# Attention over slots: both passes by blocks of 128 rows with running states, plain fp32 products on the diagonals, and a new order of the step

## The reference

```python
q, k, v, s = x @ Wq, x @ Wk, x @ Wv, clip(x @ Ws, -32, 32)   # 64, 64, 128, 64 columns a head
z = cumlogsumexp(s, time); p = exp(s - z); g = exp(z_before - z)
hk = hk * g + k (outer) p        # running state, 64 x 64
ok = q . hk                      # one row of 64 slots for each time step
pv = softmax(ok)
hv = hv * g + p (outer) v        # running state, 64 x 128
o  = pv . hv
o  = rmsnorm(o) * weight * silu(x @ Wg);  out = o @ Wo
```

## Time and profile before

| | |
|---|---|
| Median of 3 runs | 1976.25 us (1975.31 to 1977.02) |
| Profiled execution | 1975.16 us |
| Its span, first to last instruction | 1973.3 us |
| Mean granted TensorE clock | 0.995 |
| Busy: TensorE, VectorE, ScalarE, GpSimd | 99%, 69%, 39%, 31% |
| A middle step of the attention (614.90 to 651.34 us) | 36.44 us |
| The attention | to about 1216 us of the span |

### The profile page before, as it was taken

The page is one execution under the profiler, slowest core; times in us unless marked ns, Lnnn a source line. Parts: engine busy times, 40 slices in busy tenths (PEclk is TensorE's granted clock), DMA queues, the critical chain, the costliest instruction groups (busy, mean ns, idle before and its releaser), DMA issues.

```text
span 1973.3 us, 30299 instructions
## 1 busy us (share of the span) xinstructions
PE 1944.0 (99%) x11747; PEld 1430.3 (72%) x11747; DVE 1365.7 (69%) x2203; ACT 779.2 (39%) x1915; POOL 607.5 (31%) x636
## 2 busy tenths in 40 slices
PE   8999999999999999999999998999999999999998
PEld 7887888888888888878888875444444368888886
DVE  4666666666676666666666678999999965555556
ACT  3332232233232332322322332888888842222222
POOL 2142242152152152152142234244442223323232
PEclk9999999999999999999999998999999999999999
DMA  5000100100100100000000000111111111111112
GB/s 171 1 1 12 38 1 12 38 1 11 38 1 12 38 4 23 24 11 28 11 11 4 1 6 19 28 27 26 26 27 27 24 23 26 27 23 27 22 17 86
DMA packets 124988, 47.06 MB, mean 24 GB/s; under 512 B 89264, under 2 KB 116400, under 8 KB 124848
## 3 DMA queue, kind: packets, MB, share of 16 engines
q1 hardware_dynamic: 124848, 45.14, 9.3%
HBM read 32.79 MB, written 4.19 MB: 19 GB/s over the span
## 4 chain that ended last, share of the span: by engine, by line
PE 93%; ACT 3%; DVE 3%; SPq 1%; issue 1%; DMA 0%; POOL 0%; POOLq 0%; DVEq 0%; ACTq 0%
PE a_ps L66 20%; PE a_ps L68 19%; PE a_ps L67 19%; PE a_ps L1020 6%; PE a_ps L982 5%; PE a_ps L1036 4%; PE a_ps L1163 4%; PE a_ps L1176 3%; PE a_ps L1004 3%; PE a_ps L1096 2%; PE a_ps L964 2%; PE a_ps L1099 2%; PE a_ps L1102 2%; ACT x_prob L1627 2%; PE a_ps L1181 1%; PE a_ps L1135 1%
## 5 line engine op out<-in xcount | busy, mean ns | idle before, releaser
L1691 DVE TENSOR_REDUCE a_raw_qks<-a_ps 128x1 f32<-128x512 f32 x512 | 320.9, 682 | 16.5 <-PE a_ps L982 15.7
L1627 ACT ACTIVATE x_prob<-a_ps 128x512 f32<-128x512 f32 x512 | 279.8, 608 | 62.3 <-PE a_ps L1004 60.9
L66 PE MATMUL a_ps<-a_vg_hi,a_xT_lo 128*128 128x512 f32 x512 | 205.0, 400 | 0.0
L68 PE MATMUL a_ps<-a_vg_hi,a_xT_hi 128*128 128x512 f32 x512 | 199.8, 390 | 0.0
L67 PE MATMUL a_ps<-a_vg_lo,a_xT_hi 128*128 128x512 f32 x512 | 199.6, 390 | 0.0
L791 POOL TENSOR_TENSOR a_causal<-a_causal,a_mask 128x128 f32<-128x128 f32 x32 | 14.7, 460 | 558.7 <-ACT a_causal L1520 558.7
L1743 DVE SCALAR_TENSOR_TENSOR a_gate<-a_gate,a_ps 128x256 f32<-128x256 f32 x128 | 53.8, 420 | 179.9 <-ACT a_gate L1515 179.9
L66 PE MATMUL a_ps<-a_xT_hi,a_qks_lo 128*128 128x512 f32 x384 | 157.5, 410 | 0.4 <-DVE a_xT_lo L1722 0.4
L68 PE MATMUL a_ps<-a_xT_hi,a_qks_hi 128*128 128x512 f32 x384 | 150.5, 392 | 0.0
L67 PE MATMUL a_ps<-a_xT_lo,a_qks_hi 128*128 128x512 f32 x384 | 149.5, 389 | 0.0
L982 PE MATMUL a_ps<-a_xT_lo,a_xT_hi 64*128 64x512 f32 x384 | 142.9, 458 | 2.7 <-DVE a_raw_qks L1691 1.8
(11 more groups left out here) (194 smaller groups left out, 4560.9 us busy)
## 6 DMA issues: line engine op xcount, KB each, us to landing
a_raw_vg<-in_L_attn_Wv_dram SPq DMA_DIRECT2D x8, 512.0 KB, 4.6
a_raw_vg<-in_L_attn_Wg_dram SPq DMA_DIRECT2D x8, 512.0 KB, 6.4
a_raw_qks<-in_L_attn_Wo_dram SPq DMA_DIRECT2D x8, 512.0 KB, 3.7
a_xT_lo<-a_xT_lo SPq DMA_DIRECT2D x32, 128.0 KB, 2.3
x_values<-acc SPq DMA_DIRECT2D x13, 256.0 KB, 2.8
acc<-in_x_dram SPq DMA_DIRECT2D x3, 1024.0 KB, 10.1
out_dram<-acc SPq DMA_DIRECT2D x6, 512.0 KB, 2.8
f_raw_down<-in_L_ffn_down_w_dram SPq DMA_DIRECT2D x44, 64.0 KB, 2.4
```

The source lines that it names most:

```text
L66: pe.matmul(out, w_lo, x_hi, start=start, stop=False)
L68: return pe.matmul(out, w_hi, x_hi, start=False, stop=stop)
L1627: nc.scalar.activation(prob[par][:, s % 4, :], score_bank(q, s, par), ACT.Exp, scale=X_SCALE).then_inc(exp_done[par], 1)
L1691: nc.vector.tensor_reduce(nm[:, q % 2, i % 4, par, i // 4:i // 4 + 1], max_bank(u, q, i, par), AX.X, ALU.max, negate=True).then_inc(max_re ...
```

## The change

- The first pass gets running states like the second. `key_scores` multiplies only the four diagonal blocks of keys and queries, in plain fp32, into the two banks `ch`; VectorE masks them in two operations (`mask_scores`). `key_states` multiplies the keys by rows (`key_rows`) with e for the first three blocks, 64 columns each, into `ch[0]`, and VectorE adds them up (`running_key_states`). `slots` multiplies e with the masked diagonal blocks and adds, for blocks 1 to 3, the running key state times the queries.
- For the keys by rows there are three more transposes (`transpose_keys`, into `okb`) and a copy on ScalarE (`copy_key_rows`).
- Keys and queries are kept in plain fp32 (`keep_keys`, `keep_queries`); all left and right high and low parts go.
- `diagonals` uses plain fp32 products. `eT` gets a second buffer.
- GpSimd's `mask_diagonals` and ScalarE's `copy_chunks` go.
- The order changes. TensorE in a middle step: key_scores, project S, key_states, states, slots, project VG, transposes of the normalised slots, project VG+1, out_rows, project VG+2, transposes of the softmax, project_out (four tiles), project VG+3, diagonals, project K, project Q, transposes of eT, transposes of the keys, values. VectorE puts one half of the gated output of step n-1 into step n, behind the masks, and does both halves of the reciprocal with the scan. ScalarE's copies of x in steps 0 and 1 (`high_x`) stand before the copy of VG+1; in step 1 two of the four transposes of x stand behind those of the softmax.

The core of the diff:

```diff
-S, VG, Q, K = 0, 1, 5, 6
+S, VG, K, Q = 0, 1, 5, 6
...
+            def key_scores(n):
+
+                pe.wait_ge(keys_kept, n + 1)
+                pe.wait_ge(queries_kept, n + 1)
                 wait(pe, diag_masked, n)
...
+                for i in range(TT):
+                    rows = slice(i * P, (i + 1) * P)
+                    for h in range(2):
+                        mm = pe.matmul(ch[h][:, rows], keys[HALF[h], rows], queries[HALF[h], rows], start=True, stop=True)
+                mm.then_inc(scores_done, 1)
+
+            def key_states(n):
+
+                pe.wait_ge(key_rows_ready, n + 1)
+                pe.wait_ge(e_ready, n + 1)
+                pe.wait_ge(scores_masked, 2 * n + 1)
+                for i in range(TT - 1):
+                    for h in range(2):
+                        mm = pe.matmul(ch[0][HALF[h], i * DK:(i + 1) * DK], key_rows[:, i, DK * h:DK * (h + 1)],
+                                       e[:, i, DK * h:DK * (h + 1)], start=True, stop=True)
+                mm.then_inc(key_states_done, 1)
 
             def diagonals(n):
 
                 for i in range(TT):
-                    mm = blocks(ch, i, i * P, i * P, (i + 1) * P)
+                    rows = slice(i * P, (i + 1) * P)
+                    for h in range(2):
+                        mm = pe.matmul(ch[h][:, rows], eT[HALF[h], n % 2, rows], wT[HALF[h], rows], start=True, stop=True)
                 mm.then_inc(diag_done, 1)
...
             def slots(n):
 
-                pe.wait_ge(masked, 2 * n + 2)
-                pe.wait_ge(chunk_dve, 4 * n + 4)
+                pe.wait_ge(scores_masked, 2 * n + 2)
+                pe.wait_ge(e_ready, n + 1)
+                pe.wait_ge(key_rows_ready, n + 1)
                 for i in range(TT):
                     for h in range(2):
-                        mm = pe.matmul(okb[DK * h:DK * (h + 1), i * P:T], e[:, i, DK * h:DK * (h + 1)],
-                                       causal[:, h, KEY_AT[i]:KEY_AT[i] + T - i * P],
-                                       start=(i == 0), stop=(i == TT - 1))
+                        pe.matmul(okb[DK * h:DK * (h + 1), i * P:(i + 1) * P], e[:, i, DK * h:DK * (h + 1)],
+                                  causal[:, h, i * P:(i + 1) * P], start=(i == 0), stop=False, skip_group_check=True)
+                for i in range(1, TT):
+                    pe.wait_ge(key_state_ready, 3 * n + i)
+                    for h in range(2):
+                        mm = pe.matmul(okb[HALF[h], i * P:(i + 1) * P], key_state[HALF[h], i - 1, :],
+                                       queries[HALF[h], i * P:(i + 1) * P], start=False, stop=True, skip_group_check=True)
                 mm.then_inc(okT_done, 1)
...
+            def transpose_keys(m):
+                pe.wait_ge(keys_kept, m + 1)
+                wait(pe, wT_ready, m)
+                transpose4(okb, [keys[:, i * P:(i + 1) * P] for i in range(TT - 1)]).then_inc(keysT_done, 1)
```

More of the change, by code:

```diff
@@ L178, in layer_program @@
         vg_lo = sb("vg_lo", [P, KT, 4 * DV], F32R)
+        zero = sb("zero", [P, 1, 1])
         wo_hi = sb("wo_hi", [P, 2, D], F32R)
         wo_lo = sb("wo_lo", [P, 2, D], F32R)
[L181 to L185, removed]
+        queries = sb("queries", [P, T])
+        keys = sb("keys", [P, T])
+        key_rows = sb("key_rows", [P, TT - 1, P])
+        key_state = sb("key_state", [P, TT - 1, DK])
+        eT = sb("eT", [P, 2, T])
         e = sb("e", [P, TT, P])
@@ L1090, in project @@
                 mm.then_inc(proj_done, 1)
[L1092 to L1104, removed]
@@ L1195, in next_project @@
                         project(n + 1, i, b1, pair1)
-                pe.wait_ge(left_ready, 2 * n + 1)
-                pe.wait_ge(right_ready, 2 * n + 1)
-                pe.wait_ge(e_ready, n + 1)
                 into = n == NSTEP - 2
-                chunks(n)
-                last_chunk(n)
-                next_project(S, VG)
+                key_scores(n)
+                next_project(S)
+                key_states(n)
+                states(n, j)
                 slots(n)
[L1205 to L1208, removed]
+                next_project(VG)
                 pe.wait_ge(okn_ready, n + 1)
@@ L1234, in step @@
                     transpose_operands(0, 0, 3)
-                next_project(VG + 2)
+                if not first:
+                    project_out(n, pair0, (0, 1, 2, 3))
                 if into:
@@ L1493, in high_x, with keep_keys, keep_queries, copy_key_rows @@
                     nc.scalar.copy(xT_hi[:, k, b * T:(b + 1) * T], x_bank(b, k)).then_inc(xhi_ready, 1)
-            def high_left(src):
-                nc.scalar.copy(left_hi[:, :], src).then_inc(left_hi_ready, 1)
-            def high_right(src):
-                nc.scalar.copy(right_hi[:, :], src).then_inc(right_hi_ready, 1)
+            def keep_keys(src):
+                nc.scalar.copy(keys[:, :], src).then_inc(keys_kept, 1)
+            def keep_queries(src):
+                nc.scalar.copy(queries[:, :], src).then_inc(queries_kept, 1)
+            def copy_key_rows(m):
+                act.wait_ge(keysT_done, m + 1)
+                nc.scalar.copy(key_rows[:, :, :].rearrange("p i c -> p (i c)"), okb[:, 0:(TT - 1) * P])\
+                    .then_inc(key_rows_ready, 1)
             def copy_proj(m, i, b):
@@ L1516, in copy_proj @@
                                          scale=0.5).then_inc(tanh_ready, 1)
-            def copy_chunks(n, squares_of=None):
-                act.wait_ge(chunk_done, 3 * n + 1)
-                nc.scalar.copy(causal[:, 0, 0:T], ch[0]).then_inc(chunk_act, 1)
-                if squares_of is not None:
-                    square_sums(squares_of, 1)
-                act.wait_ge(chunk_done, 3 * n + 2)
-                nc.scalar.copy(causal[:, 0, CHUNK_AT[1]:CHUNK_AT[1] + T], okb).then_inc(chunk_act, 1)
             def copy_oT(n):
@@ L1554, in next_proj @@
                         copy_proj(n + 1, i, b1)
-                copy_chunks(n, None if first else n - 1)
-                act.wait_ge(chunk_done, 3 * n + 3)
-                high_left(eT[:, :])
+                if not first:
+                    square_sums(n - 1, 1)
                 into = n == NSTEP - 2
                 next_proj(S, VG)
-                if not first:
-                    copy_oT(n)
-                next_proj(VG + 1)
                 if into:
@@ L1846, in step @@
                 into = n == NSTEP - 2
[L1847 to L1850 removed]
+                mask_scores(n)
+                if not first:
+                    gated_output(n - 1, (j - 1) % B, 0)
                 clip(n + 1, b1)
[L1852 removed]
+                running_key_states(n)
+                running_states(n)
+                normalised_slots(n)
                 gating(n + 1, VG, b1)
[L1854 to L1858 removed]
                 slot_maxima(n)
[L1861 to L1862 removed]
+                less_maxima(n)
                 if at(n, 0):
```

256 lines of the change are left out of this document (93 added, 163 removed).

## The result

The changed kernel takes **1953.93 us** (median of 4 runs, 1953.27 to 1954.4), the kernel before 1976.55 us (4 runs on the same chip). The ratio is 0.9886 with a 95% interval of 0.9869 to 0.9903: faster by 22.6 us. The forecast was 1943 us with a range of 1930 to 1964. The result lies in the range, but a third of the forecast gain is missing.

What follows compares the result with a forecast made beforehand. TensorE, fully busy in the steady attention, was taken as the bound. Saving 1.10 us a step (-33.0 over 30), with ends of +3.5, -1.4, +0.1 and -2.5, gave -33.3 us: 1943 us, 8-in-10 range 1930 to 1964.

Steps and rivals of the forecast that it cites:

- Inside the steps only TensorE's own instructions count: Steady attention: TensorE fills each 36.44 us step, so only its instructions' time matters while no new wait appears.
- Price of a plain product: Narrow fp32 blocks: two passes 0.112 us apart, the same pitch as a narrow single pass; diagonals save 0.40 a step.
- key pass: Middle step: new scores take 1.11 us where the old chunks took 2.12, saving 1.01.
- Slots and states +-0: Middle step: slots and states take 3.09 us instead of 3.11, saving 0.02, with key states at 0.37.
- Rival "no overlap": Products of key state and queries run one head after the other: 0.67 us a step, 1964 us; chance 0.15.
- a chain late by a part: Either of two thin margins missed by 0.5 us: 15.5 us over 31 steps, 1958 us; chance 0.12.
- slower: Output projection waits on the low output part, over 1.95 us later than placed; late by 2.5 gives 1993; chance 0.05.
- no gain: Four-part passes cost more than three narrow ones in the scores, so no time is saved: 1976 us; chance 0.04.
- Step 0, -2.5: First step: 1.4 us less waiting, for the exponentials and left low part, plus the 1.10 saved every step.
- Step 1, +3.5: Copies of x delay the low output part: a 3.9 us wait, less the old 0.4.
- Step 30, +0.1: TensorE's wait for the maxima grows from 1.3 to 2.5 us, set against the step's saving of 1.1.
- Step 31, -2.5: Last step: loses the 1.7 us right-low-part wait, 0.4 on diagonals and 0.4 ahead of the slots.

Runs made afterwards that it cites:

- e7: Kernel before, with only the diagonals' three-part products made plain fp32 on the high parts, low parts left out: 1961.49 us, ratio 0.9924.
- e4: Changed kernel, with ScalarE copying two of the four tiles of x later in step 1, where TensorE turns them: 1945.43 us, ratio 0.9849.
- e2: Kernel before, with the feed-forward part's tiles alone placed 32 bytes higher: 1983.46 us, ratio 1.0034.
- e3: Kernel before, with the feed-forward part's tiles alone placed 64 bytes higher: 1983.63 us, ratio 1.0041.
- e9: Kernel before, with the feed-forward part's tiles placed 2048 bytes further on: 1975.77 us.
- e13: Kernel before, with all tiles of the attention and the feed-forward part moved 32 bytes together: 1975.14 us, ratio 1.000.
- e10: Kernel before, with the feed-forward part's tiles placed 512 bytes further on: 1976.63 us.
- e1: Changed kernel, with `zero` put back behind the attention's other tiles, so feed-forward tiles lie 32 bytes lower, as before: 1945.26 us, ratio 0.9841.
- e5: Changed kernel, step 30: fifth pair's maximum ahead of scan and reciprocals, first cross-attention operands turned one projection later: 1952.57 us, ratio 0.988.

## Why the prediction was right, and where it was not

- *Inside the steps only TensorE's own instructions count.* Right: no wait from 106 to 1090 us, and the step shrank by what its instructions shrank.
- *Price of a plain product: two passes 0.112 us apart.* Right. The diagonals saved 0.39 by the trace and 0.42 alone in e7, forecast 0.40. The key pass saved 1.12, or 1.06 without the 0.06 named above, forecast 1.01.
- *The Trainium skill's four passes for a true fp32 product* ("FP8 and Floating Point Precision", TensorE Precision Notes) remain no price for narrow blocks: eight pairs of passes took 1.41 us with both changes of tiling, where the twelve pairs of the three-part products took 1.80. In wide blocks the trace agrees with them. Each of the two instructions of a plain product took 0.43 us with 512 columns (old slots, from 623.17 to 623.60 us), so the product took 0.86, nearly four passes of 0.23. With 128 columns each took a quarter of that, 0.11, but a single pass of a three-part product took 0.11 there too and not a quarter of 0.23. What makes the plain product cheaper in narrow blocks is that the passes it replaces don't shrink with their columns.
- *Slots and states +-0.* They saved 0.13: key states 0.40 us (605.25 to 605.65), near the forecast 0.37 and far from the upper bound of 0.66.
- *Rival "no overlap"*: fell. The 12 passes into one bank start at 607.28 and the next instruction at 608.08, 0.80 us, as forecast for overlap (0.78); one head after the other they would need 12 x 0.112 = 1.34 by that price. The two passes of a pair start 0.007 us apart. The Trainium skill's "TensorEngine Tiling (Array Packing)" (Gotcha 1: PSUM Pressure) would have them apart; the trace does not agree.
- *Rivals "a chain late by a part", "slower", "no gain"*: fell. The output projection does not wait in any step from 2 to 29.
- *Step 0, -2.5*: measured -1.7 in this pair, but from the first projection pass on it is -3.1; the changed kernel's profiled execution came to that pass 1.4 us later. Over the seven profiles with the old order and the seven with the new one the ends of step 0 are 65.1 to 66.2 and 62.0 to 64.0 us, 2.6 apart on average, so the term stands within about 0.5.
- *Step 1, +3.5*: the wait was right (forecast 3.9, measured 3.75, at the output projection), and what follows a wait was missed: 2.8 us of half clock here (1.4 to 2.8 in three executions), gone with the wait in e4.
- *Step 30, +0.1*: too small by 3.3. The wait for the maxima is 2.8 (forecast 2.5), but the wait of 2.3 us for GpSimd's operands at the transposes of the cross attention was not in the sum. The new order turns the first operands before GpSimd has made them; no instruction of that step's cross attention is listed among those moved. These make 2.6 of the 3.3; the rest is not placed. The clock matters here too: step 30 takes 43.8 us in the profiles of the old order with full clock in it (e2, e3, e9, e13) and 45.4 in those with a stretch of half clock (before, e7, e10), and the changed kernel has such a stretch as well, a granted clock of 0.66 from 1140 to 1145 us.
- *Step 31, -2.5*: measured -3.6. Of that some 1.5 us is luck with the clock. In the kernel before, six passes from 1187.5 us on are 0.43 us apart, in the changed one none; e13, the old order without them, has 21.04 us where the kernel before has 22.56. The wait of 1.8 us for the gated output works against it.
- **The step that failed** is the sum whose terms end with step 31: -33.0 + 3.5 - 1.4 + 0.1 - 2.5. It puts the feed-forward part at nothing without a reason, and neither the list of changes nor the prediction names the move of `zero`. That part takes 8.4 us more. e1 without that shift has 1945.26 us, 2.3 above the forecast.

Sum of the misses: 8.4 (placement) + 2.3 (step 1) + 3.3 (step 30) + 0.8 (step 0) - 2.4 (middle steps, 28 x 0.085) - 1.1 (step 31) = 11.3 of the 11.4 us between 33.3 and 21.9.

That the result lies in the range is in part luck. The range was made wide for products that don't overlap and for late chains, and neither came; what used up the room was a cost that no rival names, and 3.5 us of misses the other way made it smaller.

What stays open: why feed-forward tiles that lie 32 or 64 bytes off slow the passes. Which tiles have to lie alike (operands of neighbouring passes, or what other engines read and write meanwhile) was not tried, nor any shift between 64 and 512 bytes or one inside the attention alone.

## What to carry to other kernels

Where TensorE is full, price a change by the distance between starts, per narrow pass and per change of tiling; here that gave 1.10 of 1.19 us a step. Then compare the length of every stage of the program, those that the diff does not name too, and treat a moved declaration as an edit of each tile laid out behind it: this one cost 8.7 us beside a measured gain of 22.6. A wait taken away ahead of a full queue comes back behind it; shorten the queue first (e5 alone gave nothing; with a reciprocal moved, step 31 gave 1.9 us back), and count what a wait of several us costs in clock afterwards.

## What the runs showed of the hardware

- A shift of the feed-forward part's tiles by 32 or 64 bytes against the others, at the same instructions, takes a pass of 512 columns from 389 to about 395 ns and its distance to the next from 227 to 232 ns (changed kernel, e2, e3). A shift by 512 or 2048 bytes, or of all these tiles together by 32, costs nothing (e9, e10, e13), and neither does 32 bytes inside the attention (changed kernel against e1).
- After a wait of about 3.8 us TensorE ran at its half clock level for 3 to 6 us (7, 12 and 14 passes in e1, e5 and the changed kernel), so the wait cost 5.4 to 6.9 us in all.
- Two heads on different row halves and column halves of the array (64*64), into one bank, overlap fully: 0.80 us for twelve passes of 128 columns.
- Each of the two instructions of a plain fp32 product takes time in proportion to its columns, 0.43 us with 512 and 0.11 with 128. A pass of a three-part product takes 0.23 us with 512 columns and 0.11 with 128.
